# Two slots of lead for the row maxima, and a reciprocal in four parts, in a cross-attention layer on one core

## The reference

```python
def _L1_xattn_ref(Q, K, V, W_q, b_q, W_k, b_k, W_v, b_v, W_o, b_o):
    ...
    q = _split_heads(Q @ W_q.T + b_q)
    k = _split_heads(K @ W_k.T + b_k)
    v = _split_heads(V @ W_v.T + b_v)
    scores = jnp.einsum('bhqd,bhkd->bhqk', q, k) / jnp.sqrt(jnp.float32(D_K))
    probs = jax.nn.softmax(scores, axis=-1)
    ctx = jnp.einsum('bhqk,bhkd->bhqd', probs, v)
    B, H, S, d = ctx.shape
    ctx = ctx.transpose(0, 2, 1, 3).reshape(B, S, H * d)
    return ctx @ W_o.T + b_o
...
x = x + _L1_xattn_ref(_layernorm(x, axis=-1), ctx_1024, ctx_1024, ...)
```

## Time and profile before

| | |
|---|---|
| Median of 3 runs | 5699.83 us (5697.81 to 5700.71) |
| The profiled execution | 5701.4 us, span 5699.6 us |
| Mean granted TensorE clock in it | 0.945 |
| Busy in the span: TensorE, VectorE, ScalarE, GpSimd | 88%, 53%, 39%, 19% |
| Layer with the change | from about 4300 to 5356 us of the span |

### The profile page before, as it was taken

How to read it: one execution, slowest core, us unless ns; L and a number is a source line. 1 busy time by engine, 2 the same in 40 slices (tenths; PEclk the granted TensorE clock), 3 DMA queues, 4 the chain that set the end, 5 groups by cost and what they waited for, 6 DMA issues and landing times. The chain is left out here.

```text
span 5699.6 us, 89603 instructions
## 1 busy us (share of the span) xinstructions
PE 4993.5 (88%) x37226; PEld 2856.0 (50%) x37226; DVE 3010.4 (53%) x5814; ACT 2210.3 (39%) x3527; POOL 1063.6 (19%) x660
## 2 busy tenths in 40 slices
PE   6879996999999999999899966666628999999897
PEld 3468884666666666666344432222214333333365
DVE  5767773555555555555100018777765666666360
ACT  5734332444444444444111115545413444444421
POOL 0155542110111011000000006444530000000021
PEclk9989997999999999999999988888868999999898
DMA  2311111000000000000100000000001000000122
GB/s 85 122 69 50 51 38 40 9 9 24 9 7 27 7 9 21 6 9 1 82 0 0 0 27 0 0 0 0 5 0 38 1 12 1 12 1 1 54 78 102
DMA packets 45384, 144.11 MB, mean 25 GB/s; under 512 B 6928, under 2 KB 18768, under 8 KB 38240
## 3 DMA queue, kind: packets, MB, share of 16 engines
q1 hardware_dynamic: 43472, 134.55, 6.7%
q0 software_dynamic: 1536, 4.20, 0.2%
HBM read 102.69 MB, written 36.04 MB: 24 GB/s over the span
## 5 line engine op out<-in xcount | busy, mean ns | idle before, releaser
L1471 DVE CUSTOM_DVE_ANT_0 ma_prob<-ma_ring,ma_mask 128x400 f32<-128x400 f32 (+1 forms) x1024 | 527.3, 572 | 262.1 <-PE ma_ring L1575 262.1
L1869 ACT ACTIVATE fa_prob<-fa_ring 128x512 f32<-128x512 f32 (+1 forms) x832 | 440.7, 599 | 443.6 <-PE fa_ring L2047 360.5
L1913 DVE TENSOR_REDUCE fa_part<-fa_ring 128x1 f32<-128x512 f32 x768 | 489.7, 685 | 226.2 <-PE fa_ring L2047 155.0
L2027 PE MATMUL fa_ring<-fa_K,fa_Q 32*128 32x512 f32 (+1 forms) x2048 | 536.2, 542 | 2.1
L1484 DVE COPY ma_PT<-ma_ring 128x512 f32<-128x512 f32 x512 | 341.9, 689 | 287.6 <-PE ma_ring L1585 287.2
L2047 PE MATMUL fa_ring<-fa_Qm,fa_K 32*128 32x512 f32 (+1 forms) x1664 | 468.8, 630 | 0.8 <-DVE fa_Qm L1930 0.8
L1585 PE MATMUL ma_ring<-ident,ma_prob 128*128 128x128 f32 (+1 forms) x3328 | 462.3, 280 | 6.7 <-ACT ma_prob L1430 6.7
L1599 PE MATMUL ma_pv<-ma_PT,ma_V 128*64 128x256 f32 (+1 forms) x3328 | 457.8, 393 | 0.0
L2238 PE MATMUL ffn_mid<-ffn_hid,ffn_h 128*128 128x512 f32 x1024 | 441.5, 593 | 9.7 <-DVE ffn_hid L2204 6.3
L1585 PEld LDWEIGHTS ma_ring<-ident,ma_prob 128*128 128x128 f32 (+1 forms) x3328 | 357.2, 141 | 163.6 <-issue 105.1
L1397 POOL TENSOR_SCALAR ma_diag<-ident,ma_rtotal 128x128 f32<-128x128 f32 x256 | 150.2, 606 | 1534.8 <-DVE ma_rtotal L1489 1534.8
(11 more groups left out here) (380 smaller groups left out, 7810.5 us busy)
## 6 DMA issues: line engine op xcount, KB each, us to landing
gd_rows<-gp_tile SPq DMA_DIRECT2D x16, 1024.0 KB, 4.2
gd_c_vg<-gd_rows SPq DMA_DIRECT2D x16, 1024.0 KB
moe_w<-in_moe_w SPq DMA_DIRECT2D x16, 1024.0 KB, 7.1
ma_w<-in_ma_w SPq DMA_DIRECT2D x32, 384.0 KB, 3.0
gd_rows<-gp_gate SPq DMA_DIRECT2D x16, 512.0 KB, 5.1
gd_c_qk<-gd_rows SPq DMA_DIRECT2D x16, 512.0 KB
ffn_h<-in_ffn_h SPq DMA_DIRECT2D x2, 4096.0 KB, 23.1
ma_ctxT<-in_ctxT SPq DMA_DIRECT2D x4, 1601.0 KB, 6.9
```

Source lines behind the costliest of these rows:

```text
L1471: nc.vector.tensor_tensor_reduce(prob[:, u % 2, t, h, k0:k0 + width], bank("S", u, t, n, h)[:, 0:width], mask[:, b % 2, half * 2 + t, k0:k ...
L1869: nc.scalar.activation(prob[0:n, (u * KT + kt) % PROBS, j, :], bank("scores", u, kt, j)[0:n, :], ACT.Exp, scale=SCALE).then_inc(p_ready, 1)
L1913: ins = nc.vector.tensor_reduce(part[:, t, j, n:n + 1], src[:], AX, ALU.max)
L2027: last = nc.tensor.matmul(bank("chunk", u, i)[:, at * w:(at + 1) * w], Q[rows, b % 2, g, tile * P:(tile + 1) * P], K[rows, b % 2, g, k0:k0 ...
```

## The change

Three things are done together.

- **Max products.** Every slot of every unit, from 0 to 12, holds exactly four, one to a head. They run two slots ahead (`LEAD = 2`): slot `k` makes those of round `k + 2` of the next unit, and slots 11 and 12 make rounds 0 and 1 of the unit after that. So eight of unit 1 come ahead of unit 0's first slot, and unit 14 makes none in slots 11 and 12. `part` has two halves, as the maxima of two units are on their way at once. `row_max` stands in slot 10, `shift` between the max reductions of slot 11.
- **Pieces.** One each in slots 0, 1, 3, 4, 6, 7, 8 and 9, and the 33rd in slot 10 of a batch's last unit.
- **Sums.** `add_up` moves from slot 11 to slot 2. ScalarE copies the sums from PSUM to `share` after the exponentials of block 3 (`take_sums`), and VectorE inverts `share` in place, 128 columns each in slots 6, 7, 8 and 9. The multiply on GpSimd waits for all four (`share_ready`).

```diff
-    MAX_SLOTS = KT - 2
-    LESS_SLOT, SUMS_SLOT, OUT_SLOT = KT - 2, KT - 2, KT - 1
+    LEAD = 2
+    LESS_SLOT, SUMS_SLOT, OUT_SLOT = KT - LEAD, 2, KT - 1
+    PARTS = {6: 0, 7: 1, 8: 2, 9: 3}
...
-    PATTERN = [2, 3, 0, 3, 1], [2, 3, 2, 0, 1], [2, 3, 0, 1, 0], [2, 3, 0, 1, 1], [2, 3, 0, 1]
-    PATTERNS = [0, 1, 4, 2, 3, 0, 4, 1, 2, 4, 3]
+    CHUNK = [(j, *divmod(k, NKB - 1)) if k < TB * (NKB - 1) else (j, None, NKB - 1) for k in range(KT) for j in (2, 3, 0, 1)]
+    CHUNKS = len(CHUNK)
...
-        part = s.sb("part", [P, TB, FJ, NKB])
+        part = s.sb("part", [P, 2, TB, FJ, NKB])
...
         def chunks_of(u, slot):
 
-            if u == LAST_UNIT or slot >= MAX_SLOTS:
-                return []
-            first = sum(len(PATTERN[p]) for p in PATTERNS[:slot])
-            return list(range(first, first + len(PATTERN[PATTERNS[slot]])))
+            k = slot + LEAD
+            of, k = (u + 1, k) if k < KT else (u + 2, k - KT)
+            return [(of, k * FJ + n) for n in range(FJ)] if of <= LAST_UNIT else []
...
-            counts = [{2: 1, 5: 1, 8: 1, 11: 3, 12: 2}.get(k, 0) + (k == KT - 1 and h == FG - 1) for h in range(FG) for k in range(KT)]
+            counts = [int(k in (0, 1, 3, 4, 6, 7, 8, 9)) + (k == 10 and h == FG - 1) for h in range(FG) for k in range(KT)]
...
         def _(pool):
...
-                pool.wait_ge(ring_free, nth["sums", u])
+                pool.wait_ge(share_ready, (u + 1) * TB)
...
         def _(act):
...
+            def take_sums(u):
+                act.wait_ge(ring_ready, turn["sums", u] + 1)
+                if u:
+                    act.wait_ge(att_ready, u)
+                nc.scalar.activation(share[:], bank("sums", u)[:], ACT.Copy).then_inc(act_taken, 1)
...
+                    if kt == SUMS_SLOT + 1 and u:
+                        take_sums(u - 1)
             take_output(LAST_UNIT)
+            take_sums(LAST_UNIT)
...
         def _(dve):
...
-            def invert(u):
-                await_turn("sums", u)
-                if u:
-                    dve.wait_ge(att_ready, u)
-                nc.vector.reciprocal(share[:], bank("sums", u)[:]).then_inc(ring_free, 1)
+            def invert(u, n):
+                dve.wait_ge(act_taken, nth["sums", u])
+                mine = share[:, n * P:(n + 1) * P]
+                nc.vector.reciprocal(mine, mine).then_inc(share_ready, 1)
...
             row_max(0)
+            for i in range(FJ):
+                chunk(1, i)
             shift(0)
+            for i in range(FJ):
+                chunk(1, FJ + i)
...
-                    if slot == SUMS_SLOT and u:
-                        invert(u - 1)
+                    if slot in PARTS and u:
+                        invert(u - 1, PARTS[slot])
...
-            invert(LAST_UNIT)
+            for n in range(TB):
+                invert(LAST_UNIT, n)
...
         def _(pe):
...
+            for i in range(FJ):
+                chunk(1, i)
             turn_less(0)
             for j in range(FJ):
                 scores(0, 0, j)
+                chunk(1, FJ + j)
             for u, (b, g) in enumerate(UNITS):
                 for slot in range(KT):
-                    ahead, middle, then = chunks_of(u, slot), len(chunks_of(u, slot)) - 2, block_after(u, slot)
+                    ahead, then = chunks_of(u, slot), block_after(u, slot)
                     for j in range(2):
                         if then:
                             scores(*then, j)
-                        for i in ahead[j:j + 1]:
-                            chunk(u + 1, i)
-                    for i in ahead[2:middle]:
-                        chunk(u + 1, i)
+                        for of, i in ahead[j:j + 1]:
+                            chunk(of, i)
                     if slot:
                         output(u, slot - 1)
                     elif u:
                         output(u - 1, KT - 1)
-                    for i in ahead[max(middle, 2):middle + 1]:
-                        chunk(u + 1, i)
                     if slot == LESS_SLOT and u < LAST_UNIT:
                         turn_less(u + 1)
-                    if then:
-                        scores(*then, 2)
-                    for i in ahead[max(middle + 1, 2):]:
-                        chunk(u + 1, i)
-                    if then:
-                        scores(*then, 3)
+                    for j in range(2, FJ):
+                        if then:
+                            scores(*then, j)
+                        for of, i in ahead[j:j + 1]:
+                            chunk(of, i)
```

More of the change, by code:

```diff
@@ L1790, in taker @@
         def taker(use):
-            return p_ready if use[0] == "scores" else act_taken if use[:2] == ("piece", 0) else ring_free
+            return p_ready if use[0] == "scores" else act_taken if use[0] == "sums" or use[:2] == ("piece", 0) else ring_free
         def take(*use):
```

39 lines of the change are left out of this document (18 added, 21 removed).

## The result

The changed kernel takes **5631.7 us** in the median of 4 runs (5629.7 to 5639.0), the kernel before, run beside it, 5700.3 us (5697.8 to 5703.1, 4 runs). The ratio is 0.9881, with a 95% interval of 0.9869 to 0.9892: 68.5 us or 1.2% faster. The forecast was 5636, with a range of 5614 to 5661. The profiled execution took 5629.7 us with a span of 5627.8, and its mean granted clock was 0.950 (0.945 before).

A forecast was written before the change was run, and what follows sets the result against it. TensorE's wait for a free PSUM bank was taken to bound a slot of eight products. Terms of -11, -46, -2.7, -4, +2 and -2 gave -64 us from 5699.8, a median of 5636, range 5614 to 5661.

The forecast's parts named there:

- The wait for a bank bounds a slot of eight: TensorE, slots of eight products on seven banks: one product loads late, leaving a 0.86 us hole; changed interval 3.89.
- no product is late: Rival for intervals without a projection: 3.03 and not 3.89, 68 us more saved, 5568 in all; chance 4%.
- The level filling alone buys little: Units 0 to 13 without projections: 51.8 against 52.6, 0.8 saved in each, 11 us in all.
- the projections' 46: Projection pieces one to a slot, riding in the hole: 15.3 us saved per batch, 46 us over three.
- are no longer: Slots with nine products before the change: the fifth max product rides in the hole, so they last 3.94 like eight.
- The pieces' price after: A batch's projections in the changed slots: 26.0 us; key or query 1.15, value 0.30, at slot 0 2.0 and 1.2.
- Units without pieces: A unit of 13 intervals without projections: 51.8 against 52.6, with ten plain intervals at 3.89.
- The sums' parts cost nothing: VectorE, slots 6 to 9: reciprocal parts of 0.95 each fit beside reductions and pieces, adding no time.
- VectorE falls behind: Rival for slots 6 to 9: a part costs 1.5, value slots grow 0.2 to 0.3, 14 us lost, 5650; 10%.
- the parts are the bound: Rival: a reciprocal part costs 3.36, VectorE overruns 60 slots, +114 against -64, about 5750; slower above 2.5; 3%.
- The start, "+2": Layer's start: eight earlier max products put reductions before the first shift and add a round; +2, kept at -2 to +5.
- Unit 14, the output projections, the end: Savings: 2.7 us from unit 14's eight fewer max products, 4 from three output projections, 2 at the layer's end.

The follow-up runs named there:

- sums back: The changed kernel with the sums product in slot 11 and one reciprocal of 512 columns out of its PSUM bank, as before: 5649.5 us, ratio 0.9907.
- first order: The changed kernel with unit 0's max products in the old order of heads (five-to-a-slot patterns): 5639.7 us, ratio 0.9888.

## Why the prediction was right, and where it wasn't

- **The wait for a bank bounds a slot of eight.** Right: 3.84 with eight turns, 2.91 with seven, and the late load where it was said to be. The Trainium skill, TensorEngine Tiling (Array Packing), Theoretical Speedup, gives up to four times for 32 rows; the runs agree in that three or four products side by side take one round. The rival *no product is late*, 3.03 a slot, came about with seven turns only, and at 2.91: two rounds in a row take 1.92 and not 0.97 + 1.07.
- **"The level filling alone buys little", 11 us; the projections' 46.** This step failed, in both halves and in opposite directions. The prediction prices a piece before by its batch (41.3 us, right) and after by eight-product slots (nearly right), and calls the difference the new places', though it names "a half whose successor had five max products" beside them. The runs: filling and lead alone 36 us (34.1 in the regular part, some 24 of it in intervals with pieces), places 12 to 17, the places without the filling -15. The failing sentence is that slots with nine products "are no longer": true only without a piece. 5.88 for 5.04 stood in the trace, in the intervals of slots 2 and 5. The 11 us, too, were given to the wrong edit: of unit 12's 1.33, the filling brings 0.35 and the move of the sums 0.98.
- **The pieces' price after**: 26.0 a batch was forecast, 29.6 measured (batch 0's 234.24 less 4 times 51.24, and 0.34 for unit 0, which has no sums). The largest miss is slot 9: a piece costs 0.5 more there than elsewhere, as the first half with short max products takes 1.56 and not 1.07 (in unit 3 from 4585.43 to 4586.99).
- **Units without pieces**: 0.8 forecast, 1.33 measured. The ten plain intervals are 3.84 and 3.82, not 3.89, which is 0.5 of the missing 0.6 (51.8 forecast, 51.24 measured); the turn of the shifts is 0.1 shorter than forecast too.
- **The sums' parts cost nothing.** Right: 0.94 a part, the intervals of slots 6 to 9 are the same to 0.01 in *sums back*, which has no parts there; as one part they cost 24 us (21.2 in the regular part). The rivals *VectorE falls behind* and *the parts are the bound* needed 1.5 and 2.5 for a part.
- **The start, "+2".** Wrong in the term and in what it left out. The lead costs 0.2 and not 2 (with the clock's reservation above). The change also gave unit 0's max products another order, which the prediction doesn't price: -6.3.
- **Unit 14, the output projections, the end**: 3.0, 3.4 and 1.9, for 2.7, 4 and 2. The term of the projections has a slip: 32 times half of 1.91 / 4 is 7.6 and not 7, and with 7.6 it would have been 2 and not 4. The end is not a sharp term: it is 43.1 in the changed kernel and 44.2 in *first order*, whose end is the same code.
- **The total is partly luck.** The pieces save 10.5 less than forecast (35.5 for 46). Against that, the units give 7.6 more, the start without its piece 8.1 more, and 3.2 came from the clock in unit 11 and from the layers ahead, which no term foresaw. The wait for a bank, the intervals with a piece and the free parts were right; that the sum is within 5 us is not owed to them alone.
